# A fused attention and feed-forward block over sixteen batches: LayerNorm 2's last steps moved ahead of two low parts, copies put behind stored sums, a clearing in two halves, and high products ahead of low ones in the output groups

## The reference

```python
xn = (x - mean(x)) / sqrt(var(x) + 1e-5)
# attention branch: 16 heads of 16, linear attention
q, k, v = split(xn @ W_qkv.T + b_qkv);  q = elu(q) + 1;  k = elu(k) + 1
kv = k.T @ v;  out = (q @ kv) / clip(q . sum(k), 1e-6)      # per head
out = out @ W_proj.T + b_proj
out = (out - mean) * rsqrt(var + 1e-5) * gamma + beta + xn    # "LayerNorm 2"
# feed-forward branch: ternary weights, a scale for each output
h = silu(xn @ w1.T * s1) * (xn @ w2.T * s2)                   # 256 -> 1024
h = gelu(h @ h1.T * t1);  h = gelu(h @ h2.T * t2)             # 1024 -> 1024, twice
result = x + out + h @ w3.T * s3                              # 1024 -> 256
```

## Time and profile before

| | us |
|---|---|
| median of 3 runs | 1481.9 |
| lowest and highest | 1480.41 and 1482.11 |
| the profiled execution, its own time | 1483.11 |
| its span, first to last instruction | 1481.0 |
| PE busy | 1462.3 |
| DVE busy | 1189.8 |
| ACT busy | 926.1 |

### The profile page before, as it was taken

The page is one execution under the profiler, slowest core; times in us unless marked ns, Lnnn a source line. Parts: engine busy times, 40 slices in busy tenths (PEclk is TensorE's granted clock), DMA queues, the critical chain, the costliest instruction groups (busy, mean ns, idle before and its releaser), DMA issues.

```text
span 1481.0 us, 33333 instructions
## 1 busy us (share of the span) xinstructions
PE 1462.3 (99%) x11020; PEld 1271.2 (86%) x11020; DVE 1189.8 (80%) x2208; ACT 926.1 (63%) x1727; POOL 359.1 (24%) x464
## 2 busy tenths in 40 slices
PE   9999999999999999999999999999999999999998
PEld 5988979979798897988979889798897979979797
DVE  6847978789787897978878788897878978789786
ACT  4555666766566675665756667566675666766564
POOL 2203214132140321303223041320413204132130
PEclk9999999999999999999999999999999999999999
DMA  8787845728366382764718548184481845727363
GB/s 236 234 287 246 295 139 198 245 88 284 112 228 216 118 286 77 242 207 145 271 61 274 180 146 306 35 287 161 163 280 51 291 141 196 246 88 264 127 202 114
DMA packets 89090, 287.66 MB, mean 194 GB/s; under 512 B 9696, under 2 KB 55392, under 8 KB 65760
## 3 DMA queue, kind: packets, MB, share of 16 engines
q0 software_dynamic: 43296, 231.75, 47.2%
q1 hardware_dynamic: 44928, 54.29, 11.2%
q10 hardware_dynamic: 832, 1.18, 0.2%
HBM read 270.42 MB, written 25.17 MB: 200 GB/s over the span
## 4 chain that ended last, share of the span: by engine, by line
PE 69%; DVE 10%; issue 10%; ACT 9%; DVEq 1%; ACTq 0%
PE ps L1032 38%; PE ps L1005 8%; PE ps L1003 7%; ACT values_out L1371 4%; PE ps L1067 4%; DVE partial_sums L1752 3%; PE ps L892 2%; ACT hidden_out L1348 2%; PE ps L955 2%; PE ps L944 2%; PE ps L893 2%; PE ps L894 2%; DVE zkv L1637 1%; ACT relu_tmp L1384 1%; ACT L1383 1%
## 5 line engine op out<-in xcount | busy, mean ns | idle before, releaser
L1032 PE MATMUL ps<-operands_a,hidden_weights 128*128 128x256 f32 x2520 | 348.6, 282 | 0.0
L1032 PE MATMUL ps<-lo_a_in_bits,hidden_weights 128*128 128x256 f16 x2520 | 323.5, 273 | 0.0
L1032 PEld LDWEIGHTS ps<-operands_a,hidden_weights 128*128 128x128 f32 x2520 | 317.8, 188 | 0.3
L1032 PEld LDWEIGHTS ps<-lo_a_in_bits,hidden_weights 128*128 128x128 bf16 x2520 | 241.1, 98 | 30.2
L783 POOL DMA_DIRECT2D hidden_weights<-weight_blocks x236 | 127.8, 541 | 566.4 <-PE ps L1032 539.0
L1702 DVE SCALAR_TENSOR_TENSOR lo_a_in_bits<-values_a,operands_a 128x512 f16<-128x512 f32 x315 | 214.8, 705 | 37.6 <-ACT operands_a L1343 26.5
L1709 DVE SCALAR_TENSOR_TENSOR lo_out_in_bits<-values_out,hidden_out 128x512 f16<-128x512 f32 x120 | 78.8, 688 | 103.8 <-ACT hidden_out L1348 103.8
L1005 PE MATMUL ps<-xnT,w_ffn 128*128 128x512 f32 x512 | 150.5, 421 | 0.0
L1032 PE MATMUL ps<-operands_b,hidden_weights 128*128 128x256 f32 x840 | 140.5, 289 | 2.0 <-DVE gate_ring L1752 1.9
L1343 ACT ACTIVATE operands_a<-values_a 128x512 fp32r<-128x512 f32 x180 | 111.3, 627 | 38.2 <-POOL values_a L758 17.4
L1297 ACT ACTIVATE gate_ring<-ps,vectors 128x512 f32<-128x512 f32 x128 | 85.9, 683 | 67.2 <-PE ps L1003 47.7
(11 more groups left out here) (165 smaller groups left out, 2839.1 us busy)
## 6 DMA issues: line engine op xcount, KB each, us to landing
hidden_weights<-weight_blocks POOLq DMA_DIRECT2D x180, 1024.0 KB, 5.3
hidden_weights<-weight_blocks POOLq DMA_DIRECT2D x60, 512.0 KB, 5.3
raw_weights<-weight_blocks SPq DMA_DIRECT2D x70, 231.5 KB, 4.4
hidden_weights<-in_w_ffn POOLq DMA_DIRECT2D x16, 512.0 KB, 8.4
weight_blocks<-weight_sums SPq DMA_DIRECT2D x16, 512.0 KB, 4.8
weight_blocks<-in_w_ffn SPq DMA_DIRECT2D x16, 512.0 KB, 11.0
out_dram<-acc SPq DMA_DIRECT2D x31, 256.0 KB, 2.2
x<-in_H SPq DMA_DIRECT2D x15, 512.0 KB, 6.5
```

The lines of the kernel that those rows point to most:

```text
L1032: r = mm(bank[:, m * HT:(m + 1) * HT], wk, xk, start=i in firsts and begins and m == 0 and j == 0, stop=i in lasts and ends and m == 1 and ...
```

## The change

Four edits:

- In the loop, VectorE runs LayerNorm 2's gain and shift, its sum and the fill of ones right behind `add_c21`, ahead of piece five of the check and the two low parts of C21. Before, gain, shift and sum came behind the low parts.
- In `out_group` the list of steps now has the four high blocks first, then the four low blocks.
- In tile 0, SyncE waits for the four stored sums of the last set ahead of the first `copy_blocks`.
- `clear_low` clears in two instructions of half the width.

```diff
@@ SyncE, first_body
                 store_sums(3)
+                for n in range(4):
+                    sp.wait_ge(s_stored[SETS - 1][n], 16)
                 copy_blocks(0)
@@ TensorE, out_group
-                    steps = ((0, c1, 0), (0, c2, 0), (0, c2, 1), (0, c1, 1), (1, c2, 1), (1, c2, 0), (1, c1, 0), (1, c1, 1))
+                    steps = ((0, c1, 0), (0, c2, 0), (1, c1, 0), (1, c2, 0), (0, c1, 1), (0, c2, 1), (1, c1, 1), (1, c2, 1))
@@ VectorE, clear_low
-                v.memset(low[:], 0).then_inc(s_low0, 1)
-                dve.wait_ge(s_low0, 1)
+                for cols in (slice(0, CHECK_COLS // 2), slice(CHECK_COLS // 2, CHECK_COLS)):
+                    v.memset(low[:, cols], 0).then_inc(s_low0, 1)
+                dve.wait_ge(s_low0, 2)
@@ VectorE, body
                     add_c21(t, 3)
+                    if more:
+                        ln2_gain_and_shift(t)
+                        ln2_sum(t)
+                        put_ones(t + 1)
                     if checking and more:
                         check_piece(t - 1, 4)
-                    if more:
-                        put_ones(t + 1)
                     lo_of_output(t, 0, "C21", first > 0)
                     lo_of_output(t, 1, "C21", first > 0)
                     if more:
-                        ln2_gain_and_shift(t)
-                        ln2_sum(t)
                         z_step(t + 1, 0)
```

## The result

| | before | changed |
|---|---|---|
| median | 1481.43 us (4 runs) | 1467.86 us (4 runs) |
| lowest to highest | 1480.41 to 1482.11 | 1467.27 to 1467.92 |
| ratio, 95% interval | | 0.9905, 0.9893 to 0.9917 |
| span of the profiled execution | 1481.0 | 1465.7 |

The changed kernel is faster by 13.6 us between the medians. The forecast was 1466.8, and 15.1 us of gain. Between the two profiled executions the difference is 15.3 us. That these two differ, 13.6 and 15.3, turns out to be the point at which the forecast went wrong.

A forecast was written before the change was run, and what follows sets the result against it. TensorE, busy 99% of the span, bounds the kernel and recurrently waits for VectorE's z steps. Gains of 14.2 + 0.1 + 0.8 = 15.1 us, from the median 1481.9, give 1466.8 us; range 1463.0 to 1472.5.

The forecast's parts named there:

- LayerNorm 2's move: Loop: filling VectorE's 3.74 us hole removes TensorE's waits for z steps, 1.04 us in 13 turns, 0.66 in tile 14.
- Order of steps: Output groups: high products before low save 0.01 us in output half 0, 14 times, 0.1 us in all.
- Copies and `w_out`: Tile 0: copies behind the stored sums let `w_out` land at least 0.7 us sooner; 0.8 us taken, between 0 and 1.0.
- Clearing: Second clearing instruction on VectorE adds 0 to 0.44 us, all inside 0.99 us of idle time: cost 0.
- the last one of the sum: End of the sum: 15.1 us off the profiled 1483.11 gives 1468.0; taken from the median 1481.9 it gives 1466.8.
- (a): Gate products: VectorE or ScalarE paces a stretch, part of the wait moves; 1474 us if half returns; chance 0.09.
- (b): VectorE's hole doesn't hold the moved work, z step 0 stays late, all but 1 us lost: 1481 us; chance 0.03.
- (c): Check piece six's load comes late, delaying `phi_k`; TensorE stops over 2 us in 14 turns: about 1495 us; chance 0.03.
- (d): Tile 15: new timing removes TensorE's 1.92 us stop for VectorE, more gain than forecast: 1465 us; chance 0.03.

The follow-up runs named there:

- the two kernels with additions: Changed kernel plus three or six unread 128x1024 VectorE additions per turn behind LayerNorm 2's sum: 1466.52 us with three, 1530.46 us with six (one run).
- the rectifier first: Changed kernel with ScalarE reading the bank of Q step 1 (two activations) ahead of the first high part of C21: 1465.44 us.
- the other three parts: Changed kernel with LayerNorm 2's steps put back behind the low parts of C21, the other three edits kept: 1481.06 us.
- z step 0 first: Kernel before with only z step 0 moved ahead of LayerNorm 2's gain, shift and sum, which stay behind the low parts: 1482.13 us.
- the rectifier with the late check: Changed kernel with ScalarE's rectifier ahead of C21's first high part, and tile 15's LayerNorm 2 and last check moved later in the output group: 1467.58 us.

## Why the prediction was right, and where it was off

**LayerNorm 2's move, 14.2 us: right, with its mechanism.** Alone it measures 14.1, by the medians. In the profile, from the first gate product of tile 1 to that of tile 15, it took 1272.36 us before and 1258.31 after, 14.05 us less, against 14.3 with the order of steps. Each part of the working has its row: the hole filled, the second low part unmoved, both waits gone, the stretch at 6.54. The usual distance between turns fell from 90.87 to 89.84, 1.03 where 1.04 was counted. (One turn took 91.16 before; 90.00 and 89.95 occur after.) The last one, out of tile 14, fell from 90.84 to 90.11, 0.73 where 0.66 was counted.

**Order of steps, 0.1: as far as can be seen.** 16 high products take 293.29 - 291.38 = 1.91 us, or 119 ns each; 16 low ones 295.04 - 293.29 = 1.75, or 109. Over the turns output half 1 takes 3.64 to 3.65 and half 0 3.65 to 3.66, where both took 3.66 without a wait. The Trainium skill (TensorE: Matmul & The Clock Gate, the back-to-back issue gap) gives one figure for 256 columns at full clock, 262 cycles or 109 ns, with no type beside it: the low products agree, the high ones don't.

**Copies and `w_out`, 0.8: the faster landing right, the gain not there.** The transfer sped up by 3 us. But the term was priced from a stop of 0.73 us with "issue" behind it, which the three other kernels with the old order of copies don't have. The medians can't decide it: the copies alone gave 0.4 us, and the interval holds 0 and 0.8.

The Trainium skill (DMA: Bandwidth & Descriptors, queues, rings and completion order) has each DMA engine take turns between the queues with work. The prediction set beside its sum what this might mean: that copies issued earlier on another queue hardly matter, and 9.7 us would stay. That reading failed. Issued 5 us ahead they cost the load some 3 us more than issued 0.6 us ahead. Turns between queues may still be what happens; no run here shows how the engines were shared.

**Clearing, 0: right.**

**The step that failed is the last one of the sum.** It read "It lies 1.2 us above the median of 1481.9, and taken from the median the forecast is 1466.8". The whole 15.1 was taken from the median, but 0.8 of it was part of what put the profiled execution above the median. A loss that helps to explain why one profile is slow must not be subtracted from a median that need not have it. Split by stretches, the difference of 15.3 between the two profiled executions is this:

| | us |
|---|---|
| start of the span to PE's first K/V product: 10.94 before, 11.50 after | -0.56 |
| from there to tile 1's gate products: 107.71 and 106.74, the stop for `w_out` | 0.97 |
| to tile 15's gate products | 14.05 |
| from there to the end | 0.84 |

Only the third row is the kernel's. The first spreads from 10.57 to 11.70 over all the profiled executions, whatever the kernel. The second is in no other execution. The last goes mostly with whether the clock fell in tile 15: where the end of the kernel has its old order, this stretch took 89.57 to 89.94 us in the five profiles with a fall, and 89.13 to 89.55 in the four without. With the third row alone the forecast from the median is 1481.9 - 14.05 = 1467.8; the median was 1467.86. That these agree to 0.1 us is luck in part, since the fourth run of before put its median at 1481.43, and from there it is 1467.4.

**The rivals.** (a) no: the turns keep what the stretch gained (1.05 there, 1.03 in the whole turn). (b) no: the hole held all three instructions. (c) no: no piece of the check waits for its load in the loop. (d), tile 15's stop of 1.92 us, stayed in the changed kernel (1.9), but it did go away in the two kernels with additions, below. What the prediction didn't look at is the wait of 1.1 us in the same tile; it is in two of the kernels with the old order too, and so is no effect of the change.

## What to carry to other kernels

An engine that idles first and is late afterwards, in every turn, can be mended by order alone. Measure the hole and the work: here 3.74 us fitted into 3.74. Moving one waited-for step ahead without filling the hole gained nothing.

Before a stop that occurs once in a profile is given a price, see whether it is in a second execution; and take from the median only what recurs.

When a step is moved later, list everything that reads its result, down to a one-column product.

## What the runs showed of the hardware that I had not expected

**The clock falls behind a short stop, in some executions and not in others.** In tile 15 all kernels but the two with additions have a stop of 1.8 to 2.3 us for `gate_ring`. The table by stretches behind it (columns as above), in the kernel with the rectifier first and in the changed one:

```profile
1434.90:1439.20 4.30, 4.30 (x24) 3.33 (x25) 4.10 (x7) 3.20 (x6) 0.53 (x1) 0.62 0.20 80
```
```profile
1438.00:1442.00 4.00, 3.93 (x35) 3.61 (x36) 4.00 (x8) 3.20 (x6) 0.53 (x1) 1.00 0.28 94
```

24 matmuls in 4.3 us at a clock of 0.62, against 35 in 4.0 at full: partly at the 1.2 GHz level, partly at 2.4. PE had been busy throughout before the stop in both. Twelve profiled executions have this stop. In those of before, LayerNorm 2's move alone, the other three parts, z step 0 first, the rectifier first, and the rectifier with the late check the clock fell behind it; in the other six it did not. The length of the stop doesn't tell them apart: 1.75 to 1.99 us with a fall, 1.83 to 2.31 without. What does, no row shows. A fall costs less than it takes: with the clock down, PE comes later to the first output product and no longer waits 1.1 us for `hidden_out` there, so the tail of before and that of the changed kernel differ by only 0.84 us.

**A stop that moves with the code.** The stop for `gate_ring` comes from VectorE, which stood still for some 2.4 us in front of that addition with nothing that the profile shows to wait for. The changed kernel's VectorE, and the one with three additions:

```profile
1437.33 0.69 DVE L1754 TENSOR_TENSOR gate_ring<-gate_ring,ps 128x512 f32<-128x512 f32 x1 [2.42 <-issue]
```
```profile
1432.13 0.69 DVE L1705 SCALAR_TENSOR_TENSOR lo_a_in_bits<-values_a,operands_a 128x512 f16<-128x512 f32 x1 [2.56 <-issue]
```

In the second the stand-still is in front of an earlier instruction, for whose result PE didn't wait, and the median was 1.3 us below that of the changed one although the kernel had more to do. Every profile of this document has one such gap of 2.3 to 3.1 us on VectorE in tile 15; in the twelve without additions it is in front of the same instruction, in the two with them it is elsewhere. What VectorE waits for there no row shows, and no run was made to find it, so it stays open.
